# First attention: probabilities and values as f16 halves, probabilities turned by DMA

## The reference, cut to what matters

```
ln_out = layernorm(layernorm(x)) * w + b                      # per token, 512
q, k, v, qx = linears of fp8(ln_out);  kx, vx = linear of the context
q, k, qx, kx = layernorm per head (128 wide), times w, plus b
core = softmax(q k' / sqrt(128)) v;  xout = softmax(qx kx' / sqrt(128)) vx
x1 = x + linear(fp8([core, xout] / smooth))                   # 8 key heads, 2 query heads to each, twice
```

## Time and profile before

| | us |
|---|---|
| median of three runs | 3307.08 |
| profiled execution | 3308.09 |
| its span, first to last instruction | 3305.9 |

### The profile page before, as it was taken

How to read it: one execution, slowest core, us unless ns; L and a number is a source line. 1 busy time by engine, 2 the same in 40 slices (tenths; PEclk the granted TensorE clock), 3 DMA queues, 4 the chain that set the end, 5 groups by cost and what they waited for, 6 DMA issues and landing times. The chain is left out here.

```text
span 3305.9 us, 57383 instructions
## 1 busy us (share of the span) xinstructions
PE 2887.7 (87%) x16324; PEld 1656.1 (50%) x16325; DVE 1797.5 (54%) x5172; ACT 1695.5 (51%) x4502; POOL 1740.7 (53%) x2429
## 2 busy tenths in 40 slices
PE   4699999999999969999999997699899999634996
PEld 2366666666666635555555543344444444322663
DVE  3366656656666555343433444588888887321331
ACT  5577777777777623223332333466666666311332
POOL 6467766776677435345544543655555655241222
PEclk9899999999999989999999998899999999757998
DMA  6601100010011055445544565355545555327444
GB/s 239 223 27 36 49 29 29 35 51 29 29 35 45 30 192 155 134 134 160 153 135 133 159 183 134 74 107 106 108 105 109 109 104 106 101 84 273 85 83 105
DMA packets 459854, 348.33 MB, mean 105 GB/s; under 512 B 295728, under 2 KB 366512, under 8 KB 459696
## 3 DMA queue, kind: packets, MB, share of 16 engines
q1 hardware_dynamic: 396896, 267.79, 29.0%
q0 software_dynamic: 16640, 38.05, 5.7%
q10 hardware_dynamic: 46224, 41.36, 4.2%
HBM read 194.88 MB, written 93.50 MB: 87 GB/s over the span
## 5 line engine op out<-in xcount | busy, mean ns | idle before, releaser
L437 PE MATMUL a_mm<-a_w_hi,a_xq_hi 128*128 128x512 f16 x768 | 301.9, 393 | 65.2 <-POOL a_xq_lo L885 61.5
L1646 POOL TENSOR_TENSOR e_st<-e_st,e_ws_tile 128x1024 f32<-128x1024 f32 x64 | 123.7, 1933 | 429.8 <-PE e_y L1402 418.9
L601 DVE BATCH_NORM_STATS2 a_st<-a_mm 128x6 f32<-128x128 f32 x768 | 170.7, 284 | 326.1 <-PE a_mm L438 231.6
L750 ACT ACTIVATE a_nrm<-a_mm,a_sc_t 128x128 f32<-128x128 f32 x768 | 290.4, 472 | 106.3 <-POOL a_sc_t L903 106.1
L438 PE MATMUL a_mm<-a_w_hi,a_xq_lo 128*128 128x512 f16 x768 | 303.2, 395 | 0.0
L1440 ACT ACTIVATE e_hh<-e_ha 128x512 f16<-128x512 f32 x128 | 76.3, 596 | 415.8 <-PE e_ha L1387 414.4
L1535 DVE SCALAR_TENSOR_TENSOR e_hl<-e_ha,e_hh 128x512 f16<-128x512 f32 x128 | 88.4, 691 | 352.3 <-ACT e_hh L1440 351.8
L902 POOL TENSOR_TENSOR a_sc_t<-a_sc_t,a_mhalf 128x4 f32<-128x4 f32 x192 | 202.5, 1055 | 138.3 <-DVE a_sc_t L608 138.0
L1811 PE MATMUL a_mm<-l_wh,a_src_hi 128*128 128x512 f16 x512 | 200.1, 391 | 76.0 <-DVE a_vl L1893 41.7
L1400 PE MATMUL e_y<-e_w2h,e_hh 128*128 128x512 f16 x640 | 242.6, 379 | 0.0
L1401 PE MATMUL e_y<-e_w2l,e_hh 128*128 128x512 f16 x640 | 242.6, 379 | 0.0
(11 more groups left out here) (350 smaller groups left out, 8294.6 us busy)
## 6 DMA issues: line engine op xcount, KB each, us to landing
e_st<-in_w SPq DMA_DIRECT2D x128, 512.0 KB, 4.3
disp<-a_empty SPq DMA_DIRECT2D x16, 781.5 KB, 4.1
e_st<-in_w1b SPq DMA_DIRECT2D x32, 352.0 KB, 3.1
e_xb<-disp ACTq DMA_DIRECT2D x41, 260.5 KB
disp<-a_empty SPq DMA_DIRECT2D x4, 2605.0 KB, 21.5
e_xb<-disp SPq DMA_DIRECT2D x40, 260.5 KB, 4.4
a_cx<-in_ctxT SPq DMA_DIRECT2D x32, 256.0 KB, 3.2
a_stage<-in_wprojT SPq DMA_DIRECT2D x16, 512.0 KB, 4.8
```

The costliest lines, as they stand in the source:

```text
L437: pe.matmul(out, xq_hi[:, n, c, :], w_hi[:, t, c, :], start=(c == 0), stop=False)
L750: ins = act.activation(nrm[:, n % 2, i * P:(i + 1) * P], src[:, i * P:(i + 1) * P], ACT.Identity, bias=sc_t[:, n % 2, 3, i:i + 1], scale=s ...
```

## The change

P and v are kept as two f16 halves each (the scaled value and what is left of it), with a factor of 1024 in p that `rsm` takes out again, and pv adds three f16 products per pair of heads instead of one f32 product. `p_high` on ScalarE stands where `p_keep` stood, `p_low` comes first in VectorE's next slot, both halves are turned by two DMAs that SP issues in that slot; `p_transpose` is gone from TensorE, and PTB is left to the x and router steps, whose waits are rewritten. pv moves from 5 to 6 slots behind its scores, o_quant from 6 to 7, out_project from 9 to 10, and all "end" steps by one slot. V copies go to a high half on ScalarE and a low half on VectorE (`v_low`).

```
+ def p_turn(b, a):                                                     # SP
+     for half, done in ((0, "p_hi"), (1, "p_lo")):
+         sp.wait_ge(sem[done], at(a, NA, b))
+         if half == 0 and not (isinstance(b, int) and b == 0 and a < 2):
+             sp.sem_inc(sem["turning"], 1)
+             sp.wait_ge(sem["pv"], at(a - 2, NA, b))
+         sp.sem_inc(sem["turning"], 1)
+         sp.dma_start_transpose(pT[half][:, a % 2, :].rearrange("p (i t) -> p i t", t=P),
+                                pq[half][:, a % 2, :]).then_inc(turned[half][a % 2], 16)
  SP plan:  - ("job", 0, weights), ("att", 5, residual), ("end", 10, store), ("in", 1, x_load)
            + ("job", 0, weights), ("att", 4, p_turn), ("att", 5, residual), ("end", 11, store), ("in", 1, x_load)
  def pv(b, a):                                                         # PE
-     pe.wait_ge(sem["p_ok"], at(a, NA, b))
+     for half in range(2):
+         pe.wait_ge(turned[half][a % 2], 16 * at(a // 2, NA // 2, b))
...
-         mm = pe.matmul(OVB[:, i * 256:(i + 1) * 256], vt[:, KV_OF[a], g * P:(g + 1) * P], pT[...], start=True, stop=True)
+         pe.matmul(OVB[:, two], vh, ph, start=True, stop=False)
+         pe.matmul(OVB[:, two], vh, pl, start=False, stop=False)
+         mm = pe.matmul(OVB[:, two], vl, ph, start=False, stop=True)
  PE plan:  - ("end", 14, r_transpose), ("end", 16, r_logits), ("end", 20, r_prefix), ...
            -  ("att", 3, p_transpose), ("att", 5, pv), ("att", 9, out_project), ("in", 6, x_transpose)
            + ("end", 15, r_transpose), ("end", 17, r_logits), ("end", 21, r_prefix), ...
            +  ("att", 6, pv), ("att", 10, out_project), ("in", 6, x_transpose)
+ def v_low(b, t):                                                      # DVE
+     if t in v_no:
...
+         dve.wait_ge(sem["v_hi"], at(v_no[t], NV, b))
+         dve.scalar_tensor_tensor(out=vt[1][:, i, :], in0=MMB[BANK[t]][:], scalar=scal[:, col:col + 1],
+                                  in1=vt[0][:, i, :], op0=ALU.mult, op1=ALU.subtract).then_inc(sem["v_ok"], 1)
+ def p_low(b, a):
+     dve.wait_ge(sem["p_hi"], at(a, NA, b))
+     if not (isinstance(b, int) and b == 0 and a < 2):
+         dve.wait_ge(turned[1][a % 2], 16 * at(a // 2 - 1, NA // 2, b))
+     dve.scalar_tensor_tensor(out=pq[1][:, a % 2, :], in0=pr[:, a % 2, :], scalar=PS, in1=pq[0][:, a % 2, :],
+                              op0=ALU.mult, op1=ALU.subtract).then_inc(sem["p_lo"], 1)
  DVE plan: - ("att", 2, row_scale), ("att", 1, smax), ("att", 6, o_quant), ("end", 10, final), ("end", 10, r_stats),
            -  x_quants, ("job", 0, stats), ("job", 0, convert), ("in", 3, x_stats),
            -  ("end", 16, r_scores), ("end", 18, r_pick), ("end", 20, r_slots)
            + ("att", 4, p_low), ("att", 2, row_scale), ("att", 1, smax), ("att", 7, o_quant), ("end", 11, final), ("end", 11, r_stats),
            +  x_quants, ("job", 0, stats), ("job", 1, v_low), ("job", 0, convert), ("in", 3, x_stats),
            +  ("end", 17, r_scores), ("end", 19, r_pick), ("end", 21, r_slots)
- def p_keep(b, a):                                                     # ACT
-     act.wait_ge(sem["ptr"], at(a, NA, b))
...
-     act.activation(pT[:, a % 2, :], PTB[:], ACT.Copy).then_inc(sem["p_ok"], 1)
+ def p_high(b, a):
+     act.wait_ge(sem["pnorm"], at(a, NA, b))
...
+     act.activation(pq[0][:, a % 2, :], pr[:, a % 2, :], ACT.Copy, scale=PS).then_inc(sem["p_hi"], 1)
  ACT plan: p_high at ("att", 3) as p_keep was; ("end", 12, r_norm), ("end", 14, r_keep), ("end", 17, r_exp) -> 13, 15, 18
  exps waits for p_lo of step a - 2 instead of its transpose
  POOL plan: - ("in", NJ, ctx_low), ("end", 11, r_scale), ("end", 21, r_scatter)] + parts
             + ("in", NJ, ctx_low), ("end", 12, r_scale), ("end", 22, r_scatter)] + parts
  x_transpose, r_transpose and r_prefix: waits for p_ok replaced by waits for the earlier users of PTB
```

More of the change, by code:

```diff
@@ L249, in layer0_attention @@
         kT = s.sb("kT", [P, 4, DM], F32)
[L250 removed]
+        vt = [s.sb(f"v{n}", [P, 4, DM], F16) for n in ("h", "l")]
         nb = s.sb("nb", [P, 2, 4], F32)
@@ L389, in store @@
                                  empty[:].unsqueeze(1).to_broadcast([P, FILL, RW])).then_inc(sem["filled"], 16)
-            run_pipeline(sp, [("job", 0, lambda b, t: weights(b, t + 1)), ("att", 5, residual), ("end", 10, store), ("in", 1, x_load)],
+            def p_turn(b, a):
[7 more added lines that the diff above has]
+                                           pq[half][:, a % 2, :]).then_inc(turned[half][a % 2], 16)
+            run_pipeline(sp, [("job", 0, lambda b, t: weights(b, t + 1)), ("att", 4, p_turn), ("att", 5, residual),
+                              ("end", 11, store), ("in", 1, x_load)],
                          NJ, SCORE_AT, head=HEAD)
@@ L401, in x_transpose @@
                 pe.wait_ge(sem["x_norm"], b + 1)
[L402 to L405, removed]
+                if isinstance(b, int) and b == 0:
                     pe.wait_ge(sem["small"], 16 * N_SMALL)
+                if not (isinstance(b, int) and b < 3):
+                    pe.wait_ge(sem["r_lg"], b - 2)
                 for c in range(KT):
@@ L461, in scores @@
                 mm.then_inc(sem["score"], 1)
[L463 to L477, removed]
-                    mm = pe.transpose(PTB[:, i * P:(i + 1) * P], pr[:, a % 2, i * P:(i + 1) * P], ident[:])
-                mm.then_inc(sem["ptr"], 1)
             def pv(b, a):
@@ L504, in out_project @@
                 mm.then_inc(sem["proj"], 1)
-            def kept(a, b):
-                return min(at(a, NA, b), NA * B) if isinstance(b, int) else at(a, NA, b)
             def r_transpose(b, k):
-                pe.wait_ge(sem["p_ok"], kept(4, b + 1))
-                if isinstance(b, int) and b == B - 1:
+                if not (isinstance(b, int) and b == 0):
                     pe.wait_ge(sem["r_pos"], b)
@@ L690, in x_quant_of @@
                 return lambda b, k: x_quant(b, n)
-            run_pipeline(dve, [("att", 2, row_scale), ("att", 1, smax), ("att", 6, o_quant), ("end", 10, final), ("end", 10, r_stats),
-                               *(("in", at_, x_quant_of(n)) for n, at_ in enumerate(X_QUANT_AT)), ("job", 0, stats),
-                               ("job", 0, convert), ("in", 3, x_stats), ("end", 16, r_scores), ("end", 18, r_pick),
-                               ("end", 20, r_slots)], NJ, SCORE_AT, ch, head=HEAD)
+            run_pipeline(dve, [("att", 4, p_low), ("att", 2, row_scale), ("att", 1, smax), ("att", 7, o_quant),
+                               ("end", 11, final), ("end", 11, r_stats),
+                               *(("in", at_, x_quant_of(n)) for n, at_ in enumerate(X_QUANT_AT)), ("job", 0, stats), ("job", 1, v_low),
+                               ("job", 0, convert), ("in", 3, x_stats), ("end", 17, r_scores), ("end", 19, r_pick),
+                               ("end", 21, r_slots)], NJ, SCORE_AT, ch, head=HEAD)
         @block.scalar
@@ L938, in _ @@
                                 ("in", 3, x_scale), ("in", 7, y_part_of(0)), ("in", 8, y_part_of(1)),
-                                ("in", NJ, ctx_low), ("end", 11, r_scale), ("end", 21, r_scatter)] + parts,
+                                ("in", NJ, ctx_low), ("end", 12, r_scale), ("end", 22, r_scatter)] + parts,
                          NJ, SCORE_AT, ch, head=HEAD)
```

39 lines of the change are left out of this document (21 added, 18 removed).

## The result

The changed kernel takes 3370.59 us in the median of four runs (3370.44 to 3372.55), the kernel before 3309.53 in the runs beside it: a ratio of 1.0188 (95% interval 1.0174 to 1.0202), slower by 61 us. The profiled execution took 3370.66 us, its span 3368.9. That is 0.6 us above the upper end of the range, and over twice the growth that was forecast.

A forecast was written before the change was run, and what follows sets the result against it. TensorE was taken to set the pace. Per batch +1.6 - 0.7 + 0.15 = +1.05, clock +0.5, so +1.55; 13 batches +20, ends +8: 3308 + 20 + 8 = 3336 us, range 3272 to 3370.

The forecast's parts named there:

- TensorE's tail: Work behind each odd slot's projection: transposes go, pv falls from 0.86 to 0.65 us; 5.2 us a batch saved.
- To the end of slot 7: From the second projection: three tails shrink, -1.95 us; a new 1.25 wait at q_transpose(3); -0.7 a batch (-1.95 to -0.3).
- Slots 8 to 15: Four tails shrink, but late row_scale(0) and GpSimd's queue delay projection 15: +0.15 us a batch (-2.6 to +0.9).
- The wait at the second projection: Slot-15 projection's end to second projection: TensorE's saving lost, the chain longer by r_scale and p_low; +1.6 us a batch.
- The r_scale in it: Four router operations on GpSimd, moved from slot 15 to slot 0 ahead of the low Q input: 1.28 us.
- the 0.3 for p_low: p_low at the head of slot 0 on VectorE meets scales on GpSimd: +0.3 us, bounds 0 and 0.69.
- The clock: The lower clock follows the second projection's idle stretch in every batch, not 7 of 13: +0.5 us a batch.
- The ends: First batch, fourth head's turn behind zero fills: +4 us (0 to 15); end, longer way per head: +4 (0 to 8).
- The DMA: Turns land 2.5 us after issue, with some 5 us spare before pv: nothing added in the steady part.
- The rival on collisions: Each of eight p_low costs GpSimd 0.69 us, 2.5 a batch beyond the forecast: 3369 us; chance 0.13.
- the one that I used: A VectorE instruction with two SBUF inputs and a GpSimd instruction lock the same port pair for their whole length.

The follow-up runs named there:

- run 13: Changed kernel with 24 extra matmuls written into the router's bank during TensorE's wait, ahead of the wait for the second projection's own bank: 3346.9 us.
- run 1: Changed kernel with r_scale put last in GpSimd's list, behind the low Q input: 3348.1 us.
- run 2: Changed kernel with final and r_stats behind statistics and v_low in VectorE's slot 15: 3364.0 us.
- run 3: Changed kernel with final and r_stats behind statistics and r_scale behind the low Q input: 3336.4 us.
- run 10: Also c3: changed kernel with p_low behind statistics, final and r_stats in slot 0 behind p_low and v_low, r_scale last on GpSimd: 3322.2 us.
- run 5: Changed kernel with every moved step back in its slot of before, the halves kept and p_low at the head of its slot: 3391.3 us.
- run 8: Changed kernel with the addition of eps to the variance moved from VectorE to GpSimd: 3384.3 us.
- run 4: Kernel before with only the slot moves (pv, o_quant, out_project, final, r_stats, r_scale, r_norm, store), without halves or DMA turns: 3414.2 us.
- run 16: Run 10's kernel with extra matmuls into the router's bank, 8 ahead of slot 0's output projection and 5 behind it: 3332.1 us.
- run 17: Run 10's kernel with x_scale in slot 4 behind scales(3) and x_norm one slot later: 3286.1 us.

## Why the prediction was wrong in size

Its direction, its bound and its kind of cause held: slower, by chains that end last while TensorE's own saving is lost. By its steps:

- *TensorE's tail*: pv 0.65, 5.2 a batch saved; right.
- *To the end of slot 7*: a new wait of 1.25 at q_transpose(3) and -0.7 in all. Measured 1.6 (the waits: 20.6 us in 13), and -0.8 with the clock set aside (26.74 in run 13 against 27.51 before). That the sum fits is luck: the wait was put 0.35 too short, and in the batches at full clock r_transpose waited 0.4 for PTB before, which I had not seen and which went with p_transpose:

```profile
PE a_ptb L516 <- ACT a_pT L787: 2.7, 7, 0.4
```

- *Slots 8 to 15*: row_scale(0) 4.9 behind the slot-7 projection, pnorm(0) 5.2, projection 15 starting at 29.0, +0.15. Measured 4.98, 5.23 (VectorE and GpSimd, below; that projection ends at 672.25), 29.2 (701.42, with its wait of 1.04) and +0.37.

```profile
677.23 0.17 DVE L626 RECIPROCAL a_ri<-a_rs 128x4 f32<-128x4 f32 x1
677.48 1.04 POOL L916 TENSOR_TENSOR a_pr<-a_pr,a_ri 128x512 f32<-128x512 f32 x1 [1.93 <-DVE a_ri L626]
```

- *The wait at the second projection*, "This segment: +1.6 (1.28 to 1.97)": this is the first term that failed. It measured +2.9. The r_scale in it was right to 0.01 (run 1), and the 0.3 for p_low was not what came on top: I moved final and r_stats by a slot without asking which statistics they would then stand ahead of, and o_quant the same. The start of statistics(15) slipped by 1.70; final and r_stats are 1.61 of VectorE there, and putting them behind took 0.70 of the segment, since row_scale then stood behind them (runs 2 and 3); with both chains clear it is 7.83 (run 10). The move was not the whole of it: with the steps unmoved the same statistics are 1.5 behind (run 5), so what I also left out is that VectorE, with its new passes, comes late to whatever stands ahead of them.
- *The clock*, "+0.5 (0 to +1.1)": the second term that failed. I let the lower level come in every batch, at its old length. It came in every batch and stayed longer: 2.3 us a batch against 0.6, so +1.7 (run 13). With 2.9, -0.8 and 0.4 that makes the 4.2.
- *The ends*, +8, from +4 in the first batch and +4 at the end: measured 11.2 - 2.9 = 8.3. The sum is right by luck: 11.2 lies within the bounds of the one part (0 to 15) but far from its 4, and -2.9 outside those of the other (0 to 8). The first batch's chain is the one that I named, with 21 us of wait in it: pv(3) waits for the turn behind the fills, o_quant(3) for pv(3), and the first x_stats went from 151.52 to 163.06. The end, where I had each head's longer way cost 4, takes 1.2 less in this stage.

```profile
155.12 0.37 PE L486 MATMUL a_ovb<-a_ph,a_vh 128*128 128x256 f16 x1 [21.26 <-DMA a_pl<-a_pql]
```

- *The DMA*: in the 13 batches the turns land 2.4 us after issue in the median, and TensorE waits for none; right, and run 5 shows what the slot of slack is for.

So 13 x (2.9 - 0.8 + 0.4 + 1.7) = 55, and 8: 63, where the forecast had 28. The rival on collisions had 3369, and its closeness is luck too, since the trace doesn't show its mechanism: p_low takes 671 to 693 ns in all 104 instructions of these batches, so nothing held it, and GpSimd's busy time rose by 1 us a batch (46.8 to 47.9), not 2.5. What is held is VectorE's passes with one SBUF input. Timeline of VectorE and GpSimd, slot 11:

```profile
688.47 2.37 DVE L599 TENSOR_SCALAR a_sc_t<-a_mv,a_eps_s 128x4 f32<-128x4 f32 x1
688.75 1.06 POOL L878 TENSOR_TENSOR a_xqs<-a_y,a_isc 128x512 f32<-128x512 f16 x1
689.75 1.05 POOL L887 TENSOR_TENSOR a_xq_hi<-a_y,a_isc 128x512 f16<-128x512 f16 x1
```

A pass over 128x4 takes 2.37 us and ends with GpSimd's second pass. Its line takes 5.71 us a batch where it took 3.58, and o_quant's two rounding passes 5.23 where they took 4.22. The Trainium skill ("SBUF — State Buffer", section "SBUF: two separate sides") names another case beside the one that I used: a VectorE instruction in a two-port mode and a GpSimd instruction exclude each other for their whole length. The trace agrees in that this pass, 2.37 for 0.23, ends with the GpSimd pass; that it runs in such a mode, and why it did not come in between the two passes of GpSimd, no run here shows. I had priced the new instruction and not the old ones that the change shifted against GpSimd. Whether the holds cost the batch by themselves stays open, as run 8 only moved them.

## What to carry to other kernels

When a step moves by a slot in in-order queues, list for every engine what then stands behind it in the new slot, and price the moved steps as well as the new ones; here each made the same chain late without the other (runs 4 and 5), and placing six steps anew (p_low, final, r_stats, r_scale, x_scale, x_norm) turned +61 us into -21. A longer wait of the bounding engine can cost, beside its length, the clock behind it, here 2.3 us a batch: a wait that is cut can pay twice, while idle matmuls in it gave the clock back in one kernel (run 13), and in another (run 16) the clock then fell at another wait.

## What the runs showed of the hardware that was not expected

- The granted clock fell at different waits in different kernels: at a 6.1-us wait in every batch of the changed kernel, at a 2.59-us wait in every second batch before, at a 2.04-us wait in ten batches of run 16; yet in ten batches of run 17 it stays at 1.00 through 1.9 and 1.0 us that follow close on each other. What decides it, these runs don't show.
- In c3 p_low itself was held, up to 1655 ns, where at the head of its slot in the changed kernel it was not in any of those batches (693 at most). That the passes of GpSimd beside it hold it there was not tested.
